# A graph network's edge stage: destination rows of all edges made by one-hot products and stored, then gathered as quads of 1 KB (416 gathers in place of 1568)

## The reference

```python
x = _layernorm(x + _L0_gnn_ref(x, edge_index, W, b))      # relu((normalised adjacency @ x) @ W + b)
x = _layernorm(x + _L1_gnn_ref(x, src, dst, U, V))        # relu(x @ U.T + (adjacency @ x) @ V.T)
x = _layernorm(x + _L2_gnn_ref(x, edge_index, 6250, W, b))# concat(mean over neighbours, x) @ W.T + b
# fourth layer, W1 is 128x64, W2 and Wg are 64x64:
pair_emb = jnp.concatenate([node_emb[src], node_emb[dst]], axis=-1)
h = jax.nn.relu(pair_emb @ W1 + b1)
interaction = h @ W2 + b2
gate = jax.nn.sigmoid(interaction @ Wg + bg)
gated = interaction * gate
summed = jax.ops.segment_sum(gated, src, num_segments=N)
pooled = summed / jnp.maximum(counts, 1.0)[:, None]       # counts: edges of each source
x = _layernorm(x + pooled)
```

## Time and profile before

| | |
|---|---|
| median of 3 runs | 4117.26 us (4117.07 to 4123.41) |
| the profiled execution | 4115.4 us, its span 4113.7 us |
| granted clock of PE, mean | 0.867 |
| busy share of the span | PE 75%, PEld 63%, DVE 57%, ACT 43%, POOL 38% |
| moved by DMA | 445 MB; read from DRAM 356 MB, written 86 MB |
| L1134, POOL's gathers in the edge stage | 1568, 1484.8 us busy |
| L729, DVE's one-hots in the adjacency stage | 2272, 577.5 us busy |

### The profile page before, as it was taken

One profiled execution on the slowest core, in us unless ns is written; L12 is line 12 of the kernel. 1 busy time (PEld: TensorE's weight loads), 2 busy tenths in 40 slices (PEclk: granted clock), 3 DMA queues, 4 the chain that ended last, 5 costly groups with the idle time before them and its releaser, 6 DMA issues.

```text
span 4113.7 us, 130778 instructions
## 1 busy us (share of the span) xinstructions
PE 3094.6 (75%) x40587; PEld 2607.2 (63%) x40588; DVE 2343.7 (57%) x7076; ACT 1769.2 (43%) x3946; POOL 1565.6 (38%) x1680
## 2 busy tenths in 40 slices
PE   6984278888886998999967677777777677767774
PEld 2442244444445988989966666776776667766774
DVE  9999899999996021021154444444444444444445
ACT  7984178888884000000033333333333333333334
POOL 1000100000000000000047777777777777777774
PEclk9987599999998999999988888788788877787777
DMA  1000012222225988988832222222222222222222
GB/s 46 4 3 1 20 80 109 109 96 107 109 109 216 361 283 304 320 310 318 272 102 56 57 55 57 56 56 56 55 56 56 55 55 57 55 56 54 56 57 44
DMA packets 182945, 444.91 MB, mean 108 GB/s; under 512 B 53003, under 2 KB 111635, under 8 KB 157039
## 3 DMA queue, kind: packets, MB, share of 16 engines
q1 hardware_dynamic: 131475, 387.96, 27.5%
q0 software_dynamic: 51040, 53.55, 6.3%
q10 hardware_dynamic: 252, 1.08, 0.1%
HBM read 356.29 MB, written 86.12 MB: 108 GB/s over the span
## 4 chain that ended last, share of the span: by engine, by line
PE 26%; POOL 18%; issue 17%; DVE 15%; DMA 15%; POOLq 4%; ACT 3%; DVEq 1%; ACTq 1%; SPq 0%; PEldq 0%
POOL x L1134 17%; PE ps L1640 16%; DMA x<-b_table,gidx 14%; DVE x L573 9%; PE ps L1614 8%; POOLq L1125 4%; DVE rows L729 4%; ACT stage L1349 1%; PE ps L1533 1%; ACT ps L1333 1%; DMA rows<-adjacency 0%; POOL x L1081 0%; DVEq L729 0%; PE ps L1701 0%; DVE x L569 0%
## 5 line engine op out<-in xcount | busy, mean ns | idle before, releaser
L1134 POOL DMA_INDIRECT x<-b_table,gidx x1568 | 1484.8, 947 | 483.8 <-issue 408.7
L1434 ACT ACTIVATE x<-ps,b1col 64x256 f32<-64x256 f32 x880 | 413.0, 469 | 962.3 <-PE ps L1797 954.5
L1614 PE MATMUL ps<-rows 128*128 128x448 bf16 x2272 | 615.6, 399 | 147.1 <-DVE rows L729 64.8
L945 DVE TENSOR_TENSOR x<-ps,x 128x256 f32<-128x256 f32 x440 | 186.8, 425 | 936.6 <-POOLq L1133 693.6
L1797 PE MATMUL ps<-ident,x 128*128 128x128 f32 x880 | 211.3, 328 | 546.0 <-DVE x L945 544.9
L1614 PEld LDWEIGHTS ps<-rows 128*128 128x128 bf16 x2272 | 328.8, 145 | 433.9 <-issue 308.7
L1806 PE MATMUL ps<-w2cat,x 128*128 128x128 f32 x3520 | 596.2, 326 | 0.0
L729 DVE TENSOR_SCALAR rows<-iota_c,x 128x448 bf16<-128x448 bf16 x2272 | 577.5, 329 | 25.2 <-PE ps L1614 23.5
L1818 PE MATMUL ps<-x 128*128 128x65 f32 x3520 | 579.7, 322 | 0.1
L1818 PEld LDWEIGHTS ps<-x 128*128 128x128 f32 x3520 | 576.2, 248 | 0.2 <-DVE x L962 0.2
L1806 PEld LDWEIGHTS ps<-w2cat,x 128*128 128x128 f32 x3520 | 553.2, 239 | 0.1
(11 more groups left out here) (274 smaller groups left out, 3048.4 us busy)
## 6 DMA issues: line engine op xcount, KB each, us to landing
rows<-adjacency SPq DMA_DIRECT2D x90, 1024.0 KB, 6.5
adjacency<-stage SPq DMA_DIRECT2D x50, 1568.0 KB, 5.2
x<-adjacency SPq DMA_DIRECT2D x60, 1024.0 KB, 6.3
x<-src_rows SPq DMA_DIRECT2D x440, 128.0 KB
rows<-adjacency SPq DMA_DIRECT2D x90, 544.0 KB, 4.9
x<-adjacency SPq DMA_DIRECT2D x60, 544.0 KB, 5.4
x<-b_table,gidx POOLq DMA_INDIRECT x1568
key_rows<-x ACTq DMA_DIRECT2D x1, 1024.0 KB, 4.4
```

The source lines that it names most:

```text
L1134: e.indirect_dma_start(out=BGT[:, s, j, :], out_offset=None, in_=b_table, in_offset=bass.IndirectOffsetOnAxis(ap=gidx[:, u * G + j:u * G + ...
L1434: ins = e.activation(pair[:, :, h, :], ps[h * D:(h + 1) * D, u, 0:2 * P].rearrange("p (a n) -> p a n", n=P), ACT.Relu, bias=b1col[h * D:(h ...
L1614: e.matmul(psf[:, bass.ds(at_bank, WIN)], hot_src[:, k // HOTS, :, k % HOTS], hot_dst[:, k % HOTS, :], start=False, stop=False, skip_group ...
```

## The change

**What is done.** The `b` row of every edge is no longer fetched by one gather per 128 edges. Each pair of a source tile and a destination tile (2401 blocks) has its edges filled up to whole quads of 4. A quad gets two places: one in source-tile order (416 x 128 places, `GR` = 416 groups of 128 quads) and one in destination-tile order (116 x 4 x 128 places, `SUPER` = 116 rounds). In destination-tile order all 128 quads of a step have their destinations in one tile, so the `b` rows come out of products of a one-hot of destinations with the tile's `b` rows in three bf16 parts. They are stored as `b_rows_all`, 59,392 rows of 1 KB. The edge stage gathers 128 quads with one indirect DMA, at the places `bx_at`. It has 460 items now.

**What comes with it.**
- POOL makes all tables, beside the adjacency stage: where each block starts (`below_bound`, with indirect DMAs), how many quads it has, running sums (`prefix`), shifts written to and read from DRAM. `settle` waits for all DMAs before it. Then 416 gathers fetch the keys of the quads (L1432).
- DVE turns the keys into ids in the middle of layer 0 (`read_quads`, `make_item_rows`); POOL scatters the destination ids to `dst_ids` (L1481, 416 scatters). Centring moves from POOL to DVE, which splits `b` in the third layer (`split_b`). The work on the old tables on DVE, PE and ACT in front of the adjacency is gone.
- The new stage of 116 rounds stands between the third layer and the edge stage, on PE, DVE, ACT and SP. `a` is scaled by ACT (50 activations) and split by POOL (`split_a`). ACT scales X behind the new stage.
- In the edge stage the one-hot of an item keeps the four edges of a quad side by side, so `edge_rows` reads its weights with a step of four columns. The ring may run three groups ahead of its landing (`GLAG` = 3).

The diff, cut to its core:

```diff
 G = 4
-GROUPS = -(-EDGES // (P * G))
+BLOCKS = NT * NT
+BCOLS = -(-BLOCKS // P)
+QUADS = EDGES // G + BLOCKS
+GROUPS = -(-QUADS // P)
 ...
-GLAG = 1
-GR = -(-GROUPS // RING) * RING
-SPAN = 7 * RING
+GLAG = 3
+SPAN = 13 * RING
 HALF_SPAN = SPAN // 2
+GR = -(-GROUPS // SPAN) * SPAN
+SLOTS_ALL = GR * P
+MAIN = GR // P
+TAILC = GR - MAIN * P
 ...
+SUPER = -(-(SLOTS_ALL + (NT - 1) * (P - 1)) // (4 * P))
 ...
 # DVE, in the layers
+            def read_quads():
+
+                cols = 104
+                for n in range(2):
 ...
+            def split_b(g):
+
+                t0, t1 = group_tiles(g)
+                e.wait_ge(dve, mark[f"p_{g}"])
+                v, parts = AGG[:, t0:t1, :], blk_rows[:, t0:t1, :]
+                rest = rest_a[:, 0, 0:t1 - t0, :]
+                q.link(e.tensor_copy(parts[:, :, 0:D], v))
+                q.link(e.tensor_tensor(rest, v, parts[:, :, 0:D], ALU.subtract))
+                q.link(e.tensor_copy(parts[:, :, D:2 * D], rest))
+                q.link(e.tensor_tensor(rest, rest, parts[:, :, D:2 * D], ALU.subtract))
+                q.mark("b_split", e.tensor_copy(parts[:, :, 2 * D:], rest))
+                e.wait_ge(dve, mark["b_split"])
 ...
+                if layer == 0:
+                    read_quads()
 ...
 # DVE, behind the layers
+            with e.Fori(0, SUPER // 4) as r:
+                for n in range(4):
+                    e.wait_ge(id_rows_in[n], r * 16 + 16)
+                    for u in range(4):
+                        e.wait_ge(spread_done, r * 16 + (4 * n + u + 1))
+                        e.tensor_scalar(ID_HOT[:, u, :], ID_ROWS[:, n, u * G * P:(u + 1) * G * P], part_f[:, 0:1], None,
+                                        ALU.is_equal).then_inc(id_hot_ready, 1)
+            for n in range(2):
+                e.wait_ge(spread_out[n], 16 * (SUPER // 2) + 16)
 ...
 # POOL, beside the adjacency
+            def settle():
+                e.wait_ge(prep_moved, 16 * moves)
+
+            def prefix(flat, n, steps):
+
+                for k in range(steps):
+                    d, a, b = 1 << k, flat[k % 2], flat[(k + 1) % 2]
+                    q.done(e.tensor_copy(b[..., 0:d], a[..., 0:d]))
+                    q.link(e.tensor_tensor(b[..., d:n], a[..., d:n], a[..., 0:n - d], ALU.add))
 ...
+            for n in range(GR):
+                if n % BATCH == 0 and n >= 2 * BATCH:
+                    e.wait_ge(quads_landed[n // BATCH % 2], 16 * BATCH * (n // BATCH // 2))
+                e.indirect_dma_start(out=quad_keys[:, G * n:G * (n + 1)], out_offset=None, in_=key_quads.rearrange("a (n j) -> (a n) j", j=G),
+                                     in_offset=bass.IndirectOffsetOnAxis(ap=key_at[:, n:n + 1], axis=0)
+                                     ).then_inc(quads_landed[n // BATCH % 2], 16)
 ...
 # POOL, from the middle of layer 0
+            e.wait_ge(ids_made, 1)
+            e.dma_start(src_full[0:MAIN * P, :].rearrange("(b p) n -> p b n", p=P),
+                        quad_keys[:, 0:G * MAIN * P].rearrange("p (b n) -> p b n", b=MAIN)).then_inc(src_stored, 16)
+            e.dma_start(src_full[MAIN * P:, :].rearrange("a n -> (a n)").rearrange("(p n) -> p n", p=P),
+                        quad_keys[:, G * MAIN * P:G * GR]).then_inc(src_stored, 16)
 ...
+            for n in range(GR):
+                if n % BATCH == 0 and n >= 2 * BATCH:
+                    e.wait_ge(ids_stored[n // BATCH % 2], 16 * BATCH * (n // BATCH // 2))
+                e.indirect_dma_start(out=dst_ids, out_offset=bass.IndirectOffsetOnAxis(ap=slot2[:, n:n + 1], axis=0),
+                                     in_=ids8[:, G * n:G * (n + 1)], in_offset=None).then_inc(ids_stored[n // BATCH % 2], 16)
 ...
+            def split_a(g):
+
                 t0, t1 = 8 * g, min(8 * g + 8, NTP)
-                xs = X[:, t0:t1, :]
-                e.wait_ge(dve, mark[f"mean{layer}_{g}"])
-                e.tensor_tensor(xs, xs, over_f(stat[:, 0, t0:t1]), ALU.add).then_inc(centred, 1)
-                e.wait_ge(centred, 2 * n + 1)
-                e.tensor_tensor(T1[:, t0:t1, :], xs, xs, ALU.mult).then_inc(centred, 1)
-
-            for layer in range(3):
-                for g in range(EG):
-                    centre(layer, g)
-
 ...
 # POOL, gather_group in the edge stage
-                for j in range(G):
-                    if j == G - 1 and (not first or s >= GLAG):
-                        e.wait_ge(b_landed[(s - GLAG) % RING], 16 * G * (rnd + (s >= GLAG)))
-                        e.sem_inc(groups_landed, 1)
-                    e.indirect_dma_start(
-                        out=BGT[:, s, j, :], out_offset=None, in_=b_table,
-                        in_offset=bass.IndirectOffsetOnAxis(ap=gidx[:, u * G + j:u * G + j + 1], axis=0)
-                    ).then_inc(b_landed[s], 16)
+                if not first or s >= GLAG:
+                    e.wait_ge(b_landed[(s - GLAG) % RING], 16 * (rnd + (s >= GLAG)))
+                    e.sem_inc(groups_landed, 1)
+                e.indirect_dma_start(
+                    out=BGT[:, s, :, :].rearrange("p j f -> p (j f)"), out_offset=None, in_=b_rows_all,
+                    in_offset=bass.IndirectOffsetOnAxis(ap=gidx[:, u:u + 1], axis=0)
+                ).then_inc(b_landed[s], 16)
 ...
 # SP, behind the layers
+            def store_spread(r, n):
+                e.wait_ge(spread_copied, 2 * r + 4)
+                e.dma_start(spread_rows[bass.ds(r, 1), :, :].rearrange("a p e -> (a p) e"), EV[:, n % 2, :]
+                            ).then_inc(spread_out[n % 2], 16)
 ...
+            with e.Fori(0, SUPER // 4 - 1) as r:
+                for n in range(4):
+                    e.wait_ge(id_hot_ready, r * 16 + (4 * n + 4))
+                    load_id_rows(r * 4 + (n + 4), n)
+                    store_spread(r * 4 + n, n)
 ...
 # ACT
+                for t in range(t0, t1):
+                    ins = e.activation(T1[:, t, :], ps[:, g % 4, (t - t0) * D:(t - t0 + 1) * D], ACT.Copy,
+                                       scale=stat[:, 0, t:t + 1])
+                ins.then_inc(a_copied, 1)
 ...
+            e.sem_inc(spread_copied, 2)
+            with e.Fori(0, SUPER // 2) as r:
+                for n in range(2):
+                    e.wait_ge(spread_out[n], r * 16 + 16)
+                    for h in range(2):
+                        e.wait_ge(spread_done, r * 8 + (4 * n + 2 * h + 2 + 4))
+                        e.activation(EV[:, n, h * 512:(h + 1) * 512], ps[:, 4 + h, :], ACT.Copy
+                                     ).then_inc(spread_copied, 1)
 ...
 # PE
+            with e.Fori(0, SUPER // 2) as r:
+                for n in range(2):
+                    e.load(tiles, spread_tab[0:1, bass.ds(r * 8 + 4 * n, 4)])
+                    for u in range(4):
+                        t = e.snap(tiles[u], min_val=0, max_val=NTP - 1)
+                        e.wait_ge(id_hot_ready, r * 8 + (4 * n + u + 1))
+                        if u % 2 == 0:
+                            e.wait_ge(spread_copied, r * 4 + (2 * n + u // 2 + 1))
+                        for j in range(G):
+                            for k in range(3):
+                                ins = e.matmul(ps[:, 4 + u // 2, (u % 2 * G + j) * D:(u % 2 * G + j + 1) * D], hot[:, u, j, :],
+                                               blk_rows[:, bass.ds(t, 1), k * D:(k + 1) * D].rearrange("p a f -> p (a f)"),
+                                               start=(k == 0), stop=(k == 2))
+                        ins.then_inc(spread_done, 1)
 ...
-                        ins = e.matmul(ps[:, 6 + s % 2, j * D:(j + 1) * D], OT[:, s % 2, j * P:(j + 1) * P],
+                        ins = e.matmul(ps[:, 6 + s % 2, j * D:(j + 1) * D], OT[:, s % 2, j:G * P:G],
                                        AT[:, s, k * D:(k + 1) * D], start=(k == 0), stop=(k == 2))
```

More of the change, by code:

```diff
@@ L1389, in _ @@
             for layer in range(3):
[L1390 to L1391 removed]
+                if layer == 0:
+                    turn_slots()
+                else:
+                    for b in (2 * layer - 2, 2 * layer - 1):
+                        turn_items(b)
                 for g in range(EG):
```

572 lines of the change are left out of this document (444 added, 128 removed).

## The result

Four runs of the changed kernel give a median of 4295.8 us (4293.7 to 4302.8), four of the kernel before 4119.7 us: ratio 1.0424, 95% interval 1.041 to 1.0437. The change makes the kernel 4.2% slower. The profiled execution of the changed kernel has a span of 4292.3 us, 178.6 us more than before.

What follows compares the result with a forecast made beforehand. POOL's gathers were taken to bound the edge stage, with DVE's loop behind. Span 4113.7 + 150 (adjacency) + 379 (new stage and around) - 251 (edge stage) = 4392, as device time 4394 us, +6.7%; range 4080 to 4660.

Steps and rivals of the forecast that it cites:

- Part 4: Adjacency stage: POOL's slot tables and quad work delay DVE, +150 us, bounds 0 and 225.
- 0.13 us for each DMA: Adjacency stage: DVE's loss for each of some 350 POOL DMAs, 45 us in all.
- Rival E: Adjacency stage: POOL's work costs DVE nothing; chance 0.1.
- Part 3 and 2: New stage of 116 rounds, 371 us, and the work around it: first edge-stage addition later by +379 us.
- 3.2 us a round: New stage: time taken for each of 116 rounds, 371 us in all, bounds 313 and 545.
- the row of 32 bytes: Adjacency's strided weight loads, +46 ns each; applied to the new stage, 255 us if PE sets the pace.
- Part 1: Edge stage: POOL drops out, DVE sets 3.7 us an item, 1698 us against 1949, -251 us.
- The 20% of items at 4.7 us: Edge stage: share of items taken as slower, PE being late when its clock is low; the rest at 3.43 us.
- Rival D: Edge and new stages: a low granted clock in both; left out of the range; chance 0.1.
- B: Edge stage: items at the 3.02 us of the unrolled ones, making the kernel faster; chance 0.15.
- Part 5: First layer and before the adjacency: quad reading, slot turning, scatters and removed table work change nothing; cover gone, 25 us.
- rival C: Layers: POOL's tables and gathers end late, so DVE and PE, or SP, wait; 4540 us; chance 0.2.

Runs made afterwards that it cites:

- e7: Kernel before, with 416 gathers of 16 bytes a partition into an unused buffer added on POOL under the adjacency stage: 4131.0 us, ratio 1.0034.
- e10: Changed kernel with one read of three registers, four new-stage rounds per turn with 16 tile numbers loaded at once, and a single key comparison on POOL: 3824.1 us, 0.9272.
- e3: Changed kernel, with DVE writing the new stage's one-hots plane by plane so that PE reads its weights contiguously: 4301.5 us, ratio 1.0441.
- e1: Changed kernel, with DVE reading group, slot and tile by one load of three registers, and one maximum replacing three bounds checks: 3838.3 us, ratio 0.9321.
- e11: Kernel before, with 390 gathers of 16 bytes a partition added on POOL, 130 ahead of the centring of each of three layers: 4174.3 us, ratio 1.0113.
- e6: Kernel before, with 60 operations of 512 columns on an unused buffer added on POOL under the adjacency stage: 4143.6 us, ratio 1.0065.
- e8: Changed kernel with one read of three registers, and PE's new-stage loop running four rounds per turn with 16 tile numbers loaded at once: 3828.5 us, 0.9296.
- e12: e10 with four buffers instead of two for the new stage's evicted rows: 3839.5 us, ratio 0.9311.

## Why the prediction was right, and where it was off

4394 us was forecast, 4296 measured, within the range, and the sign was right with the mechanism: three prices against one gain. The deviations, by the steps:

- **Part 4, POOL's tables under the adjacency, +150: +91.** The mechanism was right, the size not. I gave the operations 105 us (85% of 123), and by the starts of the same one-hots in both traces the stage had lost 84 us when the key gathers began. That is near by some luck: the operations were busy 165 us and not 123, and DVE lost half of it and not 85%. The step that failed is 0.13 us for each DMA, 45 us: the gathers under the stage cost 7 us, some 20 ns each, and 27 ns in e7. L936's mean delay beside gathers, from which I took that price, did not carry over. Rival E, that POOL's work costs DVE nothing, is out.
- **Part 3 and 2, around and in the new stage, +379: +373.** 3.2 us a round were forecast, 3.09 came; the start was 8 us late of the forecast once the shifts before it are taken off (2239.2 less 93.5 and 20 is 2126, forecast 2118). But the 3.2 were near for a partly wrong reason. In the changed kernel ACT doesn't wait for the store; PE, whose 48 products take 2.2 us and not the 1.4 that I gave them at full clock, its queue between rounds, the evictions and the one-hots hold the round. The store's 3.0 us is the bound right behind (e10). DVE's comparison of one-byte ids took 0.49 us, between the bounds. Of the weights' step, up to 255 us by the row of 32 bytes, the stage pays 2 us (e3).
- **Part 1, the edge stage, -251: -308.** Two terms were off, in opposite ways. DVE's 3.43 us is the fastest item and not the usual one: a quarter took 3.44 or less, the median is 3.55, and the four places of the unrolled loop take 3.43, 3.51, 3.58 and 3.78 us on average. That is +67 us over 459 items at 3.43. The 20% of items at 4.7 us, 124 us of the sum, never came. No run shows an item that PE holds for 4.7 us: in the kernel before it repeated its work of an item in 2.46 us where the granted clock was 1.00 (2133.08 to 2135.54 us) and in 4.60 us where it was 0.50 (3009.37 to 3013.97), and in the changed kernel the longest step between two additions is 4.24 us. The granted clock of the stage is 1.00 now, where it was 0.81 before with the same busy share of PE, 0.71 against 0.72. In e1, with PE busy 96%, it is 1.00 too. Long pauses as the 2.36 us of the earlier trace rows are gone: PE's longest wait for DVE's addition is 1.3 us from 2700 to 3700 us, where it was 3.1 from 2300 to 3300 before. That this is why the clock rose is not shown. Rival D, a low granted clock in both stages, is out (the new stage had 0.95). So is B, items at the 3.02 us of the unrolled ones, which the lower end of the range (4080) rests on: with one gather a group in place of four only 2 items in 100 take less than 3.42 us.
- **Part 5, at nothing:** the quads' gathers end at 1472 us (forecast 1470), and neither DVE nor SP waits for them; rival C is out. What I put at nothing and was not is the layers' +20 us, of which e11 accounts for half at most.

Sum of the deviations: -59 - 6 - 57 + 20 = -102 us; with +2 us of small shifts in the table it is -100, against 4296 - 4394 = -98. That the total is within 2.3% owes something to errors of both signs.

## What to carry to other kernels

A change that takes one engine off the path is worth only the distance to the next bound, so that bound should be moved in the same step: here DVE's reading of three table entries an item stood at 3.4 to 3.6 us right behind POOL's 4.44, and with it cut the change turns from 4.2% slower to 6.8% faster, while the cut alone gives nothing. Look for a bound of this kind in the queue's rows, for the waits may put it down to the engine that ended just before. Where POOL is given work "under" a DVE that is full, count long operations by their length, as the traces show it here (4.59 us of DVE beside one of 4.67), short ones of 0.6 us at about six tenths (e6: 20.3 of 33.3 us), and the gathers at almost nothing (e7: 27 ns each). And when a bound is taken away and little is gained, as with PE's branch in the new stage, read in the new trace what the engines wait for now before calling the bound no bound.

## What was not expected of the hardware

- Reading registers from an on-chip table: 0.31 us for one, 0.75 us for three on DVE (e1); 0.38 us for four on PE, 1.64 us for sixteen (e8), and 3.2 us for sixteen where four store buffers were in use (e12).
- The arithmetic and bounds check behind such a read on DVE cost 0.21 us in the queue (0.19 and 0.02), two thirds of the read.
- An address that is worked out from a register stands between PE's products: the first three of each twelve are 0.11 to 0.12 us apart, the last seven 33 ns.
- An operation of POOL can stand in the trace for 3.69 us and hold up nobody, while one of 4.67 us holds a one-hot for 4.59.
